# Perceiver layer on one core: keys and values projected by one plain fp32 product in place of three fp32r products of split parts

## The reference, cut to what matters

```python
q = query_states @ Wq.T + bq
k = key_value_states @ Wk.T + bk          # 12544 x 256 by 256 x 256
v = key_value_states @ Wv.T + bv
scores = jnp.einsum('bhqd,bhkd->bhqk', q * SCALE, k)     # per head
attn = jax.nn.softmax(scores, axis=-1)
ctx = jnp.einsum('bhqk,bhkd->bhqd', attn, v)
return ctx @ Wo.T + bo
```

## Time and profile before

| | |
|---|---|
| median of 3 runs | 576.75 us |
| the three runs | 576.61, 576.75, 581.04 us |
| span of the profiled execution | 577.4 us |
| busy: PE, PEld, DVE, ACT, POOL | 544.8, 502.4, 421.6, 330.7, 92.1 us |
| mean granted clock of TensorE | 0.985 |

### The profile page before, as it was taken

One profiled execution on the slowest core, in us unless ns is written; L12 is line 12 of the kernel. 1 busy time (PEld: TensorE's weight loads), 2 busy tenths in 40 slices (PEclk: granted clock), 3 DMA queues, 4 the chain that ended last, 5 costly groups with the idle time before them and its releaser, 6 DMA issues.

```text
span 577.4 us, 15741 instructions
## 1 busy us (share of the span) xinstructions
PE 544.8 (94%) x6460; PEld 502.4 (87%) x6460; DVE 421.6 (73%) x797; ACT 330.7 (57%) x635; POOL 92.1 (16%) x75
## 2 busy tenths in 40 slices
PE   7888989999999999999999999999998998778897
PEld 7777989999999999999999999999987877736686
DVE  5689868778777787787787877877877317866674
ACT  3423747667676676675666766766764850062463
POOL 7641101011011011110110111101000000015000
PEclk9999999999999999999999999999999999978899
DMA  6999995856977878777678787796575019920000
GB/s 196 152 158 152 182 154 97 120 119 120 129 120 115 128 121 124 118 113 129 119 114 128 121 122 118 120 125 101 78 118 175 3 38 377 375 87 1 1 1 9
DMA packets 44615, 70.41 MB, mean 122 GB/s; under 512 B 6784, under 2 KB 15104, under 8 KB 44416
## 3 DMA queue, kind: packets, MB, share of 16 engines
q1 hardware_dynamic: 44304, 69.02, 65.8%
q10 hardware_dynamic: 240, 0.39, 0.5%
HBM read 30.53 MB, written 0.13 MB: 53 GB/s over the span
## 4 chain that ended last, share of the span: by engine, by line
PE 80%; DVE 8%; DMA 6%; SPq 2%; ACT 1%; issue 1%; POOL 0%; DVEq 0%
PE bank L608 17%; PE bank L624 15%; PE bank L584 14%; PE bank L567 10%; PE bank L556 10%; DMA kT<-kst 5%; PE bank L834 3%; PE bank L850 3%; SPq L244 2%; PE bank L632 2%; DVE stepmax L946 1%; DMA qmat<-maxT 1%; PE bank L654 1%; PE bank L532 1%; PE bank L647 1%
## 5 line engine op out<-in xcount | busy, mean ns | idle before, releaser
L946 DVE TENSOR_REDUCE stepmax<-bank 128x2 f32<-128x512 f32 x392 | 262.9, 688 | 92.2 <-PE bank L584 68.7
L403 ACT ACTIVATE probs<-bank 128x512 f32<-128x512 f32 x392 | 229.8, 601 | 139.8 <-PE bank L608 135.6
L608 PE MATMUL bank<-qmat,kT 128*128 128x256 f32 x784 | 164.5, 294 | 4.2 <-DMA kT<-kst 3.4
L584 PE MATMUL bank<-kT,qM 128*128 128x256 f32 x784 | 161.2, 287 | 4.1 <-DVE stepmax L946 1.9
L608 PEld LDWEIGHTS bank<-qmat,kT 128*128 128x128 f32 x784 | 120.8, 191 | 18.9 <-issue 9.9
L584 PEld LDWEIGHTS bank<-kT,qM 128*128 128x128 f32 x784 | 121.5, 191 | 7.7 <-DVE stepmax L946 4.0
L316 POOL TENSOR_TENSOR cparts<-ctxT,cparts 128x512 fp32r<-128x512 f32 x49 | 63.4, 1294 | 326.7 <-ACT cparts L363 326.6
L556 PE MATMUL bank<-cparts,wk 128*128 128x256 f32 x588 | 101.3, 283 | 2.1 <-POOL cparts L316 2.1
L567 PE MATMUL bank<-wv,cparts 128*128 128x256 f32 x588 | 101.9, 284 | 0.7 <-ACT val L383 0.7
L624 PE MATMUL bank<-probs,val 128*17 128x128 f32 x3136 | 95.1, 273 | 0.0
L624 PEld LDWEIGHTS bank<-probs,val 128*17 128x17 f32 x3136 | 81.4, 97 | 6.5
(11 more groups left out here) (188 smaller groups left out, 320.7 us busy)
## 6 DMA issues: line engine op xcount, KB each, us to landing
kT<-kst SPq DMA_DIRECT2D x291, 128.0 KB, 4.6
ctxT<-in_ctxT SPq DMA_DIRECT2D x49, 256.0 KB, 5.5
w<-in_w SPq DMA_DIRECT2D x24, 512.0 KB, 10.0
bias<-in_biases SPq DMA_DIRECT2D x1, 1024.0 KB, 7.3
kT<-kst ACTq DMA_DIRECT2D x3, 128.0 KB, 5.0
qmat<-maxT SPq DMA_DIRECT2D x24, 8.0 KB
w_xk<-in_w_xk SPq DMA_DIRECT2D x1, 256.0 KB, 3.1
w_xq<-in_w_xq SPq DMA_DIRECT2D x1, 256.0 KB, 3.6
```

What stands on the lines that cost most here:

```text
L403: act.activation(probs[k % PROBS][:, :, :], sc_bank[k % 3][:, :].rearrange("p (h q) -> p h q", q=P), ACT.Exp).then_inc(S["exp_ready"], 1)
L584: last = pe.matmul(mx_bank[p % 2][:, a * SK:(a + 1) * SK], qM[:, p, a, :], kT[:, n % RING, p, :], start=True, stop=True)
L608: last = pe.matmul(sc_bank[k % 3][:, i * 2 * P:(i + 1) * 2 * P], kT[:, n % RING, p, j * P:(j + 1) * P], qmat[b % 2][:, p, :, :], start=Tru ...
L946: dve.tensor_reduce(stepmax[:, n - first_step(block_of(n)), 2 * p:2 * p + 2], mx_bank[p % 2][:, :].rearrange("p (a k) -> p a k", a=2), AX_ ...
```

## The change

The splits of the context and of the two weights are gone from ACT, POOL and DVE. Each half is now one plain fp32 product of the loaded context and the loaded weight, where it was three fp32r products; both halves of the features are still added in the bank. The context has 8 buffers in place of 4, in the room that the parts took, and a buffer is loaded anew when the keys and values of its old step are done, where it was when its low part was made. Two kinds of filler products are new in the tail: `keep_busy_rows` with 32 of the 128 rows of the array each, and `keep_busy_halves` with 64 rows each.

```diff
-CRING = 4
+CRING = 8
...
                 if n >= CRING:
-                    sp.wait_ge(S["cl_ready"], n - CRING + 1)
+                    sp.wait_ge(S["k_done"], n - CRING + 1)
+                    sp.wait_ge(S["v_done"], 2 * (n - CRING) + 2)
...
-            def context_low(n):
-
-                pool.wait_ge(S["ch_ready"], n + 1)
-                pool.tensor_tensor(cparts[n % 2][:, 1, :, :], ctxT[n % CRING][:, :, :],
-                                   cparts[n % 2][:, 0, :, :].bitcast(F32), ALU.subtract
-                                   ).then_inc(S["cl_ready"], 1)
...
-            def context_high(n):
-
-                act.wait_ge(S[f"ld_ctx{n % CRING}"], 16 * (n // CRING) + 16)
-                if n >= 2:
-                    act.wait_ge(S["v_done"], 2 * (n - 2) + 2)
-                act.activation(cparts[n % 2][:, 0, :, :], ctxT[n % CRING][:, :, :], ACT.Copy
-                               ).then_inc(S["ch_ready"], 1)
...
-            products = [(pw, pc, c) for pw, pc in ((0, 0), (1, 0), (0, 1)) for c in range(DC)]
+            def context_loaded(n):
+
+                pe.wait_ge(S[f"ld_ctx{n % CRING}"], 16 * (n // CRING) + 16)
...
-                for i in range(3 * half, 3 * half + 3):
-                    pw, pc, c = products[i]
-                    if (n, t, i) == (0, 0, 4):
-                        pe.wait_ge(S["cl_ready"], 1)
-                    last = pe.matmul(k_bank[:, t * SK:(t + 1) * SK], wk[:, pw, c, t * P:(t + 1) * P], cparts[n % 2][:, pc, c, :],
-                                     start=(i == 0), stop=(i == 5))
+                last = pe.matmul(k_bank[:, t * SK:(t + 1) * SK], w["xk"][:, half, t * P:(t + 1) * P],
+                                 ctxT[n % CRING][:, half, :], start=(half == 0), stop=(half == DC - 1))
...
-                for i in range(3 * half, 3 * half + 3):
-                    pw, pc, c = products[i]
-                    last = pe.matmul(v_bank[:, j * D:(j + 1) * D], cparts[n % 2][:, pc, c, j * P:(j + 1) * P], wv[:, pw, c, :],
-                                     start=(i == 0), stop=(i == 5))
+                last = pe.matmul(v_bank[:, j * D:(j + 1) * D], ctxT[n % CRING][:, half, j * P:(j + 1) * P],
+                                 w["xv"][:, half, :], start=(half == 0), stop=(half == DC - 1))
...
+            def keep_busy_rows(n):
+
+                for i in range(n):
+                    r = slice(32 * (i % 4), 32 * (i % 4) + 32)
+                    pe.matmul(B[4 + i % 4][:, 0:P], ident[r, :], ident[r, :], start=True, stop=True)
+
+            def keep_busy_halves(n, wide):
+
+                for i in range(n):
+                    r = slice(64 * (i % 2), 64 * (i % 2) + 64)
+                    if wide:
+                        pe.matmul(B[6 + i % 2][:, 0:2 * P], ident_r[r, :],
+                                  ident_r[r, :].unsqueeze(1).broadcast_to([64, 2, P]), start=True, stop=True)
+                    else:
+                        pe.matmul(B[6 + i % 2][:, 0:P], ident_r[r, :], ident_r[r, :], start=True, stop=True)
...
-            keep_busy(6)
+            keep_busy_rows(16)
             pe.wait_ge(S["dve_a_xn"], 1)
...
-            keep_busy(7)
+            keep_busy_halves(8, True)
             pe.wait_ge(S["dve_a_out"], 1)
...
-            keep_busy(6)
+            keep_busy_halves(10, False)
             pe.wait_ge(S["dve_c_xn"], 1)
```

More of the change, by code:

```diff
@@ L156, in perceiver_layer @@
         ctxT = [place(f"ctxT{i}", [P, DC, SK]) for i in range(CRING)]
-        cparts = [place(f"cparts{i}", [P, 2, DC, SK], F32R) for i in range(2)]
-        wk = place("wk", [P, 2, DC, D], F32R)
-        wv = place("wv", [P, 2, DC, D], F32R)
+        w = {n: place("w_" + n, [P, DC, D]) for n in ("xk", "xv")}
         temps_start = at[0]
@@ L165, in perceiver_layer @@
         at[0] = parts_start
-        w = {n: place("w_" + n, [P, DC, D]) for n in ("xk", "xv", "xq")}
+        w["xq"] = place("w_xq", [P, DC, D])
         qparts = place("qparts", [P, PAIRS, 2, 4, HD], F32R)
@@ L173, in perceiver_layer @@
             w[n] = place("w_" + n, [P, DC, D])
[L174 removed]
+        tail_weights_end = at[0]
+        assert tail_weights_end <= parts_start
         at[0] = arena_start
@@ L271, in _ @@
             sp.dma_start(*weight("xv")).then_inc(S["ld_v"], 16)
-            for n in range(2, CRING):
+            for n in range(2, 4):
                 ctx_load(n)
             for t in range(-2, NS + 1):
-                if CRING <= t + 6 < NS:
+                if t + 6 < NS:
                     ctx_load(t + 6)
@@ L357, in _ @@
         def _(act):
-            def context_high(n):
-                act.wait_ge(S[f"ld_ctx{n % CRING}"], 16 * (n // CRING) + 16)
-                if n >= 2:
-                    act.wait_ge(S["v_done"], 2 * (n - 2) + 2)
-                act.activation(cparts[n % 2][:, 0, :, :], ctxT[n % CRING][:, :, :], ACT.Copy
-                               ).then_inc(S["ch_ready"], 1)
             def keys_high(n):
                 act.wait_ge(S["k_done"], n + 1)
+                if n == 0:
+                    act.wait_ge(S["ld_k"], 32)
                 if n >= 2:
@@ L409, in part_out @@
                 act.activation(parts[:, b, :], pv_bank[:, :], ACT.Copy).then_inc(S["part_ready"], 1)
-            act.wait_ge(S["ld_k"], 32)
-            act.activation(wk[:, 0, :, :], w["xk"][:, :, :], ACT.Copy).then_inc(S["act_wkvh"], 1)
-            context_high(0)
             act.wait_ge(S["ld_const"], 16)
@@ L416, in _ @@
             keys_high(0)
-            context_high(1)
-            act.wait_ge(S["ld_v"], 16)
-            act.activation(wv[:, 0, :, :], w["xv"][:, :, :], ACT.Copy).then_inc(S["act_wkvh"], 1)
             first_keys_half()
@@ L446, in _ @@
                         values_out(t + 2)
-                    if q == 5 and t + 4 < NS:
-                        context_high(t + 4)
                     if q == 2:
```

32 lines of the change are left out of this document (9 added, 23 removed).

## The result

The changed kernel took 599.88 us (median of 4 runs, 597.13 to 603.07), the kernel before 576.68 us beside it (572.22 to 581.04): 1.0403 times, with an interval of 1.0353 to 1.0454. The forecast was 600 us. The profiled execution of the changed kernel took 603.07 us, its span is 601.2.

A forecast was written before the change was run, and what follows sets the result against it. PE's own work was taken to bound the main stretch. The span of 577.4 us plus 22.0 there and 1.2 at the start, 0 in the tail, gave 600.6, less 0.7 for the median: 600 us, range 596 to 606.

The forecast's parts named there:

- The main stretch: Weighted values of step 8 to step 46: PE's own work is the time, nothing else; +22.0 us.
- 0.072 us a half: Each half of keys or values: one plain product of 0.432 us replaces three fp32r of 0.360 us.
- the sign that I gave: Main stretch groups: 0.43 us from a key's or value's plain product to what follows; a group every 0.91 us.
- What lies between the steps: Step boundaries in the main stretch: PE's waits for the small DMA into qmat go away, giving back 0.2 us.
- the 22.0 that I gave: Main stretch: 308 halves at 0.072 us, 22.2 us, with 0.2 us of waits given back.
- The start: Up to step 8: step 0 starts at some 22.3 us in place of 21.87; +1.2 us, between 0.7 and 2.0.
- The query's chain through DVE is thus late by 0.1: Start, after keys(0): four plain products take 1.73 us where twelve fp32r took 1.44, delaying the query's chain by 0.1.
- The tail: After the last keys and values: three changed fillers make nothing late, the 32-row ones running four at once; 0 us.
- the rival in which the tail loses: Tail: serial filler, +1.8 us, or the clock falling, at most 1.7; together 603.5 us; chance 0.07.
- Loads setting the pace (540 or 585): PE's groups: standing operand loads set the pace, 0.72 us a group, 540 us, chance 0.02; half way 0.864, 585, 0.05.
- Crossings that cost 6 us: Main stretch: 0.02 us at each way out of a plain product, +6 us, 606 us; chance 0.04.
- the 0.7 us that the sum took off for the median: End of the sum: 0.7 us less than the 600.6 us span, as the runs' median stands to the span; 599.9.

The follow-up runs named there:

- e1_spaced: Changed kernel with POOL's fills of kT for steps 1 to 6 each held until the keys of the step before are done; 598.3 us, 1.0351 times.
- e3_plain_on_before: Kernel before with its splits kept, but each half of keys and values one plain fp32 product of the high parts; 596.59 us, 1.0351 times.
- e7_two_products: Kernel before with two fp32r products in a half in place of three, low weight by high context left out; 558.09 us, 0.9693 times.
- e2_bunched_before: Kernel before with POOL's fills of kT for steps 0 to 4 in one row ahead of the first context_low; 582.9 us, 1.0100 times.
- e12_before_free_dve: Kernel before with more plain fillers in the tail's causal attention and POOL's step 2 fill held until DVE made the query's parts; 574.05 us, 0.9930 times.

## Why the prediction was right, and which of its terms were not

- **The main stretch is PE's alone: right.** PE waits for nothing in it, and its 355.29 us hold whether ACT and POOL have work or not (e1_spaced, e3_plain_on_before).
- **0.072 us a half: nearly right.** A group was forecast at 0.91 us and is. But the sign that I gave, 0.43 from a plain product to what follows it, didn't come: it is 0.25, and the rest of the cost falls on the pair behind. Over the steps, one took 8.78 us, by the chain of before:

```profile
92.03 1.87 PE bank L624 x64
100.81 1.87 PE bank L624 x64
109.59 1.87 PE bank L624 x64
```

and takes 9.32 (102.02, 111.34, 120.66 in the chain of after): +0.54, or 0.0675 a half. 38 x 0.54 = 20.5 us.
- **What lies between the steps: mis-sized.** I counted 0.2 us of waits going away, from the earlier trace rows. 336.37 less 38 x 8.78 leaves 2.7 us that weren't the steps'; of them 1.1 are left (355.29 - 38 x 9.32). So 1.6 us came back, and the view of waits had shown 0.2 of it. The reason is taken to be that of e7_two_products, short waits that vanish in the modelled ends. 20.5 - 1.6 = 18.9, against the 22.0 that I gave, which held 4 halves outside the stretch.
- **The start: the step that failed.** "The query's chain through DVE is thus late by 0.1" looked at PE and at ACT's waits and not at what the removal of `context_low` does to POOL's queue. The fills behind it moved up into one row, held DVE for 6.2 us more and cost the clock: +9.4 us in place of +1.2. e2_bunched_before prices the row alone at 91.31 - 83.08 = 8.2, and e1_spaced the rest at 84.28 - 83.08 = 1.2. That this is the forecast's number proves little: executions of one start differ by as much, and with the plain products alone (e3_plain_on_before) step 8 starts at 81.95, 1.1 us *earlier* than before. Nor was the way to it as forecast. Step 0 came at 20.24 in e1_spaced, not at 22.3: the hold on DVE's split of the queries that e12_before_free_dve takes away is in the trace of the kernel before, in none of the rows that I read, and went with POOL's low parts (L971 takes 0.49 us for both halves in e1_spaced). PE then waited for the copies, and this gain didn't reach step 8.
- **The tail: the fillers are as forecast, the clock is not.** The fillers gain nothing (1.0031; the interval leaves room for a loss of up to 3 us, so the rival in which the tail loses isn't excluded), and four groups of rows did run at once. The 4.6 us that the profiled execution gained go with the clock: some 6 us at the lower level against some 17. The same kernel's second profile has 100.5 us, and e1_spaced's, with the same fillers, 103.5, so a part of the 4.6 is chance of the execution. With more fillers the three profiled tails are 100.3, 100.3 and 100.9 us; what decides in one execution how often the clock falls stays open.
- **Rivals.** Loads setting the pace (540 or 585) is out: a group takes 0.907 us, not 0.72 or 0.864, and the loads' busy time fell from 322 to 321 us while the stretch grew by 19. Crossings that cost 6 us are out: the group's 0.907 leaves 0.427 for a plain product in it, less than 0.432.

That forecast and result agree to 0.1 us is luck: three misses nearly cancel, and the second set of runs of the same kernel has its median at 603.67 us. So is the 0.7 us that the sum took off for the median: in every run on record the time is 1.7 to 1.9 us longer than the span, so the profiled execution of the kernel before, with a span of 577.4, took some 579.2 us, 2.5 over the median of its runs. The 0.7 is what one execution happened to give; for the changed kernel it is 1.3 (601.2 and 599.88). The kernel that the working described is e1_spaced, at 598.3 us inside the range too; of its span's +20.2 us over that of before 1.2 are at the start and 18.9 in the main stretch.

## What to carry to other kernels

Price a matmul by starts over a whole group of the loop, not by the gap behind one product or by its duration: three fp32r products of this shape (0.360 us) are cheaper than one plain fp32 product (0.43) where PE is the bound, and the work that they cost the other engines is free as long as none of these is the bound. A gain is worth less than it saves where the next limit is near: 36.5 us off PE's work brought 19.9 here. One profile is one execution; look at a second before a difference of a few us in a short tail is given a cause. When an instruction is taken out of a queue, ask what stood behind it and now moves up, and beside whom that runs. Keep GpSimd's long memsets away from a `tensor_scalar` on the path, or write that step so that it isn't held.

## What the hardware showed that was not expected

- A `tensor_scalar` of 128 x 256 from SBUF to SBUF, 0.41 us alone, took 6.57 to 6.61 us in three executions beside five memsets of 1.8 us in a row, and 3.15 in another; the same arithmetic as `scalar_tensor_tensor` took 0.48 us beside them.
- After PE's 6 us of idleness the granted clock was 0.51 over 5.5 us in which PE was busy throughout; the 8 records of keys(0) took 2.93 us there.
- Plain fp32 and fp32r products alternate at no cost that shows: the group's 0.907 us less four fp32r products at 0.120 leaves 0.427, where a plain product in a row takes 0.43. With half of the products plain the cost is half, 0.27 us of 0.54 in a step.
- In the tail, 30 more plain products put into waits of PE delayed nothing that shows, and the granted clock of the stretch was 0.97 in the three profiled executions, 0.92 in the kernel before.
